# Row factors through memory and residuals without reciprocals in a four-layer graph network

## The chip, the cores and the metric

One core of a Trainium2 chip runs the whole kernel. The metric is device microseconds of one execution, the median over runs; lower is better. TensorE (PE) multiplies into PSUM, VectorE (DVE), ScalarE (ACT) and GpSimd (POOL) work on tiles of 128 partitions, and SyncE (SP) issues most DMAs. Each engine takes its instructions in the order in which they were written; a wait at the head of a queue holds up all that stands behind it.

## What is computed

32 graphs of 256 nodes with 128 features pass four layers. Layers 0 and 1 are graph attention, layer 2 a gated attention by edge type, layer 3 a relational sum. Each layer adds its input to its result and normalizes every node (cut from the reference):

```
def _layernorm(x): return (x - mean(x)) / sqrt(var(x) + 1e-05)
# layers 0 and 1
h = x @ W.T;  s_src = h @ a_src;  s_dst = h @ a_dst
e = leaky_relu(s_src[:, :, None] + s_dst[:, None, :], 0.2)
alpha = softmax(where(adj == 0, -1e9, e), axis=-1)
out = alpha @ h
...
x = _layernorm(x + layer0(x));  x = _layernorm(x + layer1(x))
x = _layernorm(x + layer2(x));  x = _layernorm(x + layer3(x))
```

## The kernel before, in words

The 32 graphs go in 16 pairs (numbered 0 to 15). A pair passes some 40 named steps, and one table, `ORDER`, fixes by hand for each engine in which order it takes the steps of all pairs; `rows0:4` is step "rows" of layer 0 for pair 4. Up to eight pairs are in flight. A second table, `BANKS`, says which of the eight PSUM banks a product of a pair takes; a product waits until the earlier holder of its bank is freed (`freed_by`).

Layers 0 and 1 avoid the softmax over a 256 by 256 matrix of logits. The exponential of a leaky sum is the larger of two products of a row factor and a column factor; what is common to a row or a column is taken out. For a pair the steps are:

- `h` (PE, L1097): the projection, with two more columns that hold the source and destination logits; `logits` (DVE, L811 and L813) copies these two columns to `logit`.
- `gains` (ACT, L609): the exponential of 128x8 logits gives `gain`, a row factor and a column factor for every node.
- `dT` (PE, L1103), `peak` (DVE, L819), `top` (PE, L1107), `dmax` (DVE, L823): the largest destination logit, found by a transposition of 4 columns into a 4x128 row in the bank of `h`.
- `rows` (PE, L1114): four transpositions of a row factor, broadcast along the columns, so that each of the 128 partitions holds the 256 row factors of a graph in PSUM.
- `weight` (DVE, L837): four instructions a pair, each the larger of a row factor from PSUM and a column factor, times the 0/1 mask, into `wgt_all` in SBUF.
- `v`, `vals` (ACT, L615 and L625): the values, with one more column that makes the row sum come out of the same product.
- `out` (PE, L1157): the product of weights and values. Its last column is the row sum.
- `rsum`, `rinv` (DVE, L852, L854, L860): the row sum, held above a tiny number, and its reciprocal; `res` (DVE, L880) adds the product times the reciprocal to the layer's input and frees the bank of `out`.
- `stats` (DVE, L888), `var` (ACT L674, DVE L894 and L898, or POOL L565), `pow` (POOL, L535), `center` (DVE, L902), `norm` (ACT L665 and L668, POOL L549, DVE L793 and L795): the normalization.

Layer 2 has `xTa`, `score`, `sigmoid`, `umax` (L802), `alpha`, `out2` and `res2`; layer 3 has `high`, `low`, `agg`, `out3` and `res3`. POOL adds the biases (`bias`, L530) and forms the low parts (`low`, L541). POOL also issues the mask loads, SP those of `x` and `xT` and the stores of the results. At the end DVE judges flags that would start a general version of the work (`judge`, L910 to L920).

At the start POOL sets a tile of zeros (L515); with it PE runs 5 idle products (L1165, 10 instructions), once the identity matrices are there as well, and then the first projection.

## Time and profile before

| | us |
|---|---|
| median of 3 runs | 253.18 (252.33 to 253.56) |
| profiled execution, its own time | 254.48 |
| its span, first to last instruction | 251.4 |
| busy: PE, DVE, ACT, POOL | 227.2, 229.2, 189.8, 173.4 |
| mean granted clock of PE | 0.982 |
| chain that ended last | PE 55%, DVE 33%, DMA 5%, the rest 7% |

The busy time of a group of instructions is the union of their times, so that where two overlap the time counts once. The mean of a group is that of one instruction, overlap included. Idle time before an instruction is put down to what released it last. The chain that ended last is followed back from the last instruction, at each step to what it waited for.

### The profile page before, as it was taken

How to read it: one execution, taken by the hardware profiler on the slowest of the kernel's cores; microseconds unless marked ns; L12 is line 12 of the kernel's file. 1: busy time of each engine (PE TensorE's matmuls, PEld its weight loads, DVE VectorE, ACT ScalarE, POOL GpSimd, SP SyncE). 2: the span in 40 equal slices, each digit the busy share in tenths (PEclk: the TensorE clock that was granted, in tenths of full speed). 3: DMA queues.
4: the chain of work that ended last, by engine and by line, in shares of the span. 5: the costliest groups of instructions: out<-in, count | busy, mean ns of one | idle time of the engine just before them, and what ended most of it. 6: DMA issues, size and time to landing. Idle time of an engine off the chain costs nothing.

```text
span 251.4 us, 5755 instructions
## 1 busy us (share of the span) xinstructions
PE 227.2 (90%) x1745; PEld 206.6 (82%) x1745; DVE 229.2 (91%) x812; ACT 189.8 (75%) x587; POOL 173.4 (69%) x260
## 2 busy tenths in 40 slices
PE   4998899999999999999999998999999979897850
PEld 4896788987999998988898997989989968776840
DVE  0399989998999999999999999999999888999894
ACT  2497856988968998867998956996891966977752
POOL 6032049878756786789837529984797996699982
PEclk9999999999999999999999999999999979999995
DMA  6999124501452313212230300011000110100106
GB/s 180 252 262 240 52 83 86 126 4 42 83 127 39 88 18 94 104 20 68 54 116 10 117 1 33 14 42 44 1 0 3 42 44 1 43 0 3 42 1 214
DMA packets 12144, 17.56 MB, mean 70 GB/s; under 512 B 1104, under 2 KB 5968, under 8 KB 12112
## 3 DMA queue, kind: packets, MB, share of 16 engines
q1 hardware_dynamic: 9520, 12.85, 16.4%
q0 software_dynamic: 2304, 4.20, 9.9%
q8 instruction: 15, 0.25, 0.4%
q10 hardware_dynamic: 288, 0.14, 0.2%
q14 instruction: 17, 0.14, 0.2%
HBM read 17.17 MB, written 4.19 MB: 85 GB/s over the span
## 4 chain that ended last, share of the span: by engine, by line
PE 55%; DVE 33%; DMA 5%; issue 3%; ACT 2%; POOL 1%; DVEq 0%; SPq 0%; POOLq 0%
PE banks L1157 25%; PE banks L1097 8%; DVE wgt_all L837 7%; PE banks L1124 6%; DVE fstats L888 6%; DMA w<-in_L_gnn_weight 5%; PE banks L1082 4%; DVE fres_all L880 4%; DVE fres_all L868 3%; PE banks L1154 3%; DVE banks L802 3%; PE banks L1114 3%; DVE wgt_all L845 2%; PE banks L1134 2%; PE banks L1107 1%
## 5 line engine op out<-in xcount | busy, mean ns | idle before, releaser
L535 POOL TENSOR_TENSOR frstd<-fvar,minus_half 128x4 f32<-128x4 f32 x64 | 64.8, 1018 | 23.3 <-ACT fvar L674 15.5
L1157 PE MATMUL banks<-vals_all,wgt_all 128*128 128x129 f32 x512 | 63.5, 277 | 3.6 <-ACT vals_all L625 1.9
L1157 PEld LDWEIGHTS banks<-vals_all,wgt_all 128*128 128x128 f32 x512 | 59.6, 191 | 6.6 <-ACT vals_all L625 3.1
L837 DVE SCALAR_TENSOR_TENSOR wgt_all<-banks,gain,mask_all 128x256 f32<-128x256 f32 x128 | 52.6, 471 | 0.3 <-PE banks L1114 0.2
L530 POOL TENSOR_TENSOR xb_all<-xs_all,bias_cen 128x256 f32<-128x256 f32 x62 | 44.5, 737 | 9.5 <-ACT xs_all L668 4.4
L888 DVE BATCH_NORM_STATS2 fstats<-fres_all 128x6 f32<-128x256 f32 x128 | 47.5, 414 | 0.1
L668 ACT ACTIVATE xs_all<-fres_all,frstd 128x128 f32<-128x128 f32 x112 | 35.7, 409 | 0.7 <-POOL frstd L535 0.6
L1157 PE MATMUL banks<-xs_all,wgt_all 128*128 128x128 f32 x256 | 32.7, 283 | 2.6 <-DVE wgt_all L845 2.5
L1157 PEld LDWEIGHTS banks<-xs_all,wgt_all 128*128 128x128 f32 x256 | 30.7, 196 | 3.8 <-DVE wgt_all L845 3.7
L1124 PE MATMUL banks<-fxT,fxTa 128*128 128x256 f32 x128 | 30.3, 381 | 0.0
L605 ACT COPY fxT<-banks 128x256 f32<-128x256 f32 x64 | 20.3, 382 | 12.7 <-PE banks L1082 12.7
L1124 PEld LDWEIGHTS banks<-fxT,fxTa 128*128 128x128 f32 x128 | 23.1, 190 | 2.7
L868 DVE SCALAR_TENSOR_TENSOR fres_all<-banks,xb_all 128x512 f32<-128x512 f32 x32 | 21.5, 679 | 3.5 <-PE banks L1157 2.1
L1114 PE MATMUL banks<-ident,gain 128*128 128x128 f32 x128 | 19.7, 279 | 1.6 <-ACT gain L609 1.2
L802 DVE TENSOR_TENSOR banks<-banks,wgt_all 128x512 f32<-128x512 f32 x32 | 20.9, 687 | 0.3
L641 ACT ACTIVATE wgt_all<-banks 128x512 f32<-128x512 f32 x32 | 19.3, 603 | 2.3 <-PE banks L1124 2.1
L541 POOL TENSOR_TENSOR fxTa<-xs_all,fxTa 128x256 f16<-128x256 f32 x28 | 18.2, 671 | 3.6 <-ACT fxTa L648 3.6
L845 DVE SCALAR_TENSOR_TENSOR wgt_all<-banks,mask_all 128x512 f32<-128x512 f32 x32 | 20.4, 678 | 0.0
L1134 PE MATMUL banks<-mask_all,fxTa 128*128 128x256 bf16 x128 | 16.8, 273 | 3.6 <-POOL fxTa L541 2.1
L1097 PE MATMUL banks<-w_fast,xT_all 128*128 128x130 f32 x128 | 19.4, 299 | 0.5 <-DVE w_fast L740 0.3
L625 ACT ACTIVATE vals_all<-banks,fscale 128x128 f32<-128x128 f32 x64 | 18.1, 377 | 2.0 <-POOL fscale L570 1.1
L642 ACT ACTIVATE banks<-banks 128x512 f32<-128x512 f32 x32 | 19.5, 609 | 0.0
(93 smaller groups left out, 419.2 us busy)
## 6 DMA issues: line engine op xcount, KB each, us to landing
xT_all<-x_turned SPq DMA_DIRECT2D x16, 256.0 KB, 2.9
mask_all<-adj_turned POOLq DMA_DIRECT2D x16, 256.0 KB, 6.0
x_all<-x_laid SPq DMA_DIRECT2D x16, 256.0 KB, 2.8
out<-xs_all SPq DMA_DIRECT2D x16, 256.0 KB, 2.2
bias<-biases_laid SPq DMA_DIRECT2D x1, 128.0 KB, 12.0
w_pack<-W_and_columns ACTq DMA_DIRECT2D x1, 68.0 KB, 3.2
w_fast<-W_turned ACTq DMA_DIRECT2D x1, 64.0 KB, 3.6
w_nat<-in_L_gnn_W SPq DMA_DIRECT2D x1, 64.0 KB, 8.3
```

What stands on the lines that cost most here:

```text
L530: nc.gpsimd.tensor_tensor(xb(u)[:, :, :], xs(u)[:, :, :], bias_cen[:, int(l) - 2, :, :], ALU.add).then_inc(fast_pool[k], 1)
L535: nc.gpsimd.tensor_tensor(frstd[:, int(l), slot(n), :], fvar[:, int(l), slot(n), :], minus_half[:, :, :], ALU.pow).then_inc(fast_pool[k], 1)
L668: last = nc.scalar.activation(xs(u)[:, b, :], fres(u)[:, b, :], ACT.Copy, scale=frstd[:, int(l), u, b:b + 1])
L802: nc.vector.tensor_tensor(scored, scored, wgt(u), ALU.max).then_inc(fast_dve[k], 1)
L837: last = nc.vector.scalar_tensor_tensor(out=wgt(u)[:, c, :], in0=place(f"rows{l}", u), scalar=gain[:, u, c, 1:2], in1=maskT(u)[:, c, :], o ...
L845: nc.vector.scalar_tensor_tensor(out=wgt(u), in0=scored, scalar=1.0, in1=maskT(u), op0=ALU.add, op1=ALU.mult).then_inc(fast_dve[k], 1)
L868: nc.vector.scalar_tensor_tensor(out=fres_all[:, pair(n, FRES), :, :], in0=gathered, scalar={"2": 0.5, "3": 1.0}[l], in1=xb_all[:, pair(n, ...
L888: nc.vector.bn_stats(fstats[:, u, :, :].rearrange("p b k -> p (b k)"), fres(u)[:, :, :].rearrange("p b d -> p d b")).then_inc(fast_dve[k], 1)
L1097: last = nc.tensor.matmul(place(f"h{l}", u)[:, b * HC:(b + 1) * HC], (xT_in if l == "0" else fxT)(u)[:, b * P:(b + 1) * P], w_fast[:, int( ...
L1114: last = nc.tensor.transpose(place(f"rows{l}", u)[:, b * P:(b + 1) * P], gain[:, u, b, 0:1].to_broadcast([P, P]), ident[:, :])
L1124: last = nc.tensor.matmul(place("score", u)[:, c * N:(c + 1) * N], fxTa(u)[:, c * P:(c + 1) * P], fxT(u)[:, :], start=True, stop=True)
L1157: last = nc.tensor.matmul(place(f"out{l}", u)[:, b * width:(b + 1) * width], wgt(u)[:, c, b * P:(b + 1) * P], (vals if l in "01" else xs)( ...
```

## The change

1. **Row factors.** Pairs 3 to 15 no longer use `rows` on PE. `dT` transposes the source logits as well, ACT takes their exponential from PSUM as a 4x128 row (`rowx`), SP writes it to memory (`rowa`, 2 KB) and reads it back for all 128 partitions into `rows_all` in SBUF (`rows` on SP, 256 KB). `weight` reads `rows_all` in the place of a PSUM bank. There are 13 pairs in 2 layers, so 26 such steps, with 52 DMAs on SP.
2. **Residuals.** In layers 0 and 1 the residual is kept times the row sum: input times row sum plus product. `rinv` falls away, and `rsum` in layer 0. The normalization takes the factor out again, if the small constant under its root is multiplied by the squared row sum: ACT forms that square (`sq`, two 128x2 instructions a pair and layer), and `var` on DVE adds it. The bank of `out` is now freed by `sq`.
3. **Start.** DVE sets the zeros, PE waits for them alone and runs 7 idle products. The first four `x` loads wait for `h0`, and the mask loads run 3 pairs ahead, not 6.
4. **New orders** on all engines, new banks, and three places with 5 idle products each on PE (`warm`). Single steps pass to other engines: DVE has `var0` 16 times (before 4), `var2` 5 (1), `var3` 4 (5), `bias3` 3 (1), `norm1` 0 (1), `norm3` 1 (2), `low` 1 (2), `fscale` 4 (5). ACT has `norm1` 6 (8), `norm3` 15 (14), `var3` 9 (2), no `var0` (5). POOL has `norm1` 10 (7), 6 `var` (24), `low` 15 (14), `bias3` 13 (15).

```diff
-AHEAD = 6
+AHEAD = 3
+ROWS, ROW_OUT = 3, 2
...
     "pe": (
-        "h0:0 h0:1 dT0:0 rows0:0 dT0:1 top0:0 top0:1 rows0:1 out0:0 out0:1 turn:0 xT1:0 h0:2 h1:0 xT1:1 dT0:2 dT1:0 "
+        "h0:0 h0:1 dT0:0 rows0:0 turn:0 top0:0 dT0:1 h0:2 rows0:1 dT0:2 top0:1 out0:0 top0:2 h0:4 rows0:2 warm:5 xT1:0 "
...
             def load_x(l, n, k):
                 if n >= X_IN:
                     sp.wait_ge(fast_dve[(n - X_IN) % K], at("dve", "res0", final(n - X_IN)))
+                else:
+                    sp.wait_ge(fast_pe[n], at("pe", "h0", final(n)))
...
+            def send_row(l, n, k):
+                q = SPREAD[l].index(n)
+                sp.wait_ge(fast_act[k], at("act", f"rowx{l}", n * H))
+                sp.dma_start(row_scratch[int(l), n].rearrange("(a d) -> a d", d=P), row_tile(l, n)).then_inc(fast_row_out[int(l)][q % ROW_OUT], 16)
+
+            def spread_rows(l, n, k):
+                q = SPREAD[l].index(n)
+                sp.wait_ge(fast_row_out[int(l)][q % ROW_OUT], 16 * (q // ROW_OUT) + 16)
+                if q >= ROWS:
+                    m = SPREAD[l][q - ROWS]
+                    sp.wait_ge(fast_dve[m % K], at("dve", f"weight{l}", final(m)))
+                sp.dma_start(rows_all[:, int(l), q % ROWS, :], row_scratch[int(l), n].rearrange("(a d) -> a d", a=1).to_broadcast([P, H * N])).then_inc(fast_rows_in[int(l)][q % ROWS], 16)
...
+            def exponential_rows(l, n, k):
+                q = SPREAD[l].index(n)
+                act.wait_ge(fast_pe[k], at("pe", f"dT{l}", n * H))
+                if q >= ROW_OUT:
+                    act.wait_ge(fast_row_out[int(l)][q % ROW_OUT], 16 * (q // ROW_OUT))
+                nc.scalar.activation(row_tile(l, n), place(f"h{l}", final(n))[0:H * NB, 260:260 + P], ACT.Exp, scale=SLOPE - 1).then_inc(fast_act[k], 1)
...
+            def squares(l, n, k):
+                act.wait_ge(fast_dve[k], at("dve", f"res{l}", final(n)))
+                for u in graphs(n):
+                    sums = place(f"out{l}", u)[:, 0:NB * (D + 1)].rearrange("p (b c) -> p b c", b=NB)[:, :, D]
+                    last = nc.scalar.activation(fsq[:, int(l), u, :], sums, ACT.Square, scale=math.sqrt(EPS))
+                last.then_inc(fast_act[k], 1)
...
             def weights(l, n, k):
-                dve.wait_ge(fast_pe[k], at("pe", f"rows{l}", final(n)))
+                spread = n in SPREAD[l]
+                if spread:
+                    q = SPREAD[l].index(n)
+                    dve.wait_ge(fast_act[k], at("act", f"gains{l}", n * H))
+                    dve.wait_ge(fast_rows_in[int(l)][q % ROWS], 16 * (q // ROWS) + 16)
+                else:
+                    dve.wait_ge(fast_pe[k], at("pe", f"rows{l}", final(n)))
...
-                        last = nc.vector.scalar_tensor_tensor(out=wgt(u)[:, c, :], in0=place(f"rows{l}", u), scalar=gain[:, u, c, 1:2],
+                        last = nc.vector.scalar_tensor_tensor(out=wgt(u)[:, c, :], in0=rows_in(l, u) if spread else place(f"rows{l}", u), scalar=gain[:, u, c, 1:2],
                                                               in1=maskT(u)[:, c, :], op0=ALU.max, op1=ALU.mult)
...
-                        last = nc.vector.scalar_tensor_tensor(out=fres(u)[:, b, :], in0=sums[:, b, 0:D], scalar=finv[:, u, b:b + 1],
-                                                              in1=(x_in if l == "0" else fres)(u)[:, b, :], op0=ALU.mult, op1=ALU.add)
+                        last = nc.vector.scalar_tensor_tensor(out=fres(u)[:, b, :], in0=(x_in if l == "0" else fres)(u)[:, b, :],
+                                                              scalar=sums[:, b, D:D + 1] if l == "0" else fsum[:, u, b:b + 1],
+                                                              in1=sums[:, b, 0:D], op0=ALU.mult, op1=ALU.add)
...
-                if l == "1":
-                    nc.vector.scalar_tensor_tensor(out=var, in0=squares, scalar=1 / D, in1=fvar[:, 0, slot(n), :],
+                if l in "01":
+                    dve.wait_ge(fast_act[k], at("act", f"sq{l}", n * H))
+                    nc.vector.scalar_tensor_tensor(out=var, in0=squares, scalar=1 / D, in1=fsq[:, int(l), slot(n), :],
                                                    op0=ALU.mult, op1=ALU.add).then_inc(fast_dve[k], 1)
...
-            pe.wait_ge(ident_set, 2)
-            pe.wait_ge(ident_bf_set, 2)
...
             pe.wait_ge(zero_set, 1)
-            idle_products(5)
+            idle_products(7, 5)
             projection_columns()
+            pe.wait_ge(ident_set, 2)
+            pe.wait_ge(ident_bf_set, 2)
```

**DVE, around the residuals of layer 1 of the first pairs.** `frow`, `fsum` and `finv` are row sums and reciprocals, `fsq` the squares from ACT. Before:

```order
L852 TENSOR_SCALAR frow<-banks 128x2 x2
L819 TENSOR_REDUCE top<-banks 4x1
L860 RECIPROCAL finv<-frow 128x4
L880 SCALAR_TENSOR_TENSOR fres_all<-banks,finv,x_all 128x128 x4
L888 BN_STATS fstats<-fres_all 128x6 x2
L854 SCALAR_TENSOR_TENSOR fsum<-banks,frstd 128x2 x2
L811 COPY logit<-banks 128x4 x2
L860 RECIPROCAL finv<-fsum 128x4
L823 TENSOR_REDUCE minus_dmax<-banks 128x1
L880 SCALAR_TENSOR_TENSOR fres_all<-banks,finv,fres_all 128x128 x4
```

Now:

```order
L890 SCALAR_TENSOR_TENSOR wgt_all<-rows_all,gain,mask_all 128x256 x4
L904 TENSOR_TENSOR fsum<-banks,frstd 128x2 x2
L890 SCALAR_TENSOR_TENSOR wgt_all<-rows_all,gain,mask_all 128x256 x4
L927 SCALAR_TENSOR_TENSOR fres_all<-fres_all,fsum,banks 128x128 x4
L936 BN_STATS fstats<-fres_all 128x6 x2
L904 TENSOR_TENSOR fsum<-banks,frstd 128x2 x2
L943 SCALAR_TENSOR_TENSOR fvar<-fstats,fsq 128x4
L927 SCALAR_TENSOR_TENSOR fres_all<-fres_all,fsum,banks 128x128 x4
L936 BN_STATS fstats<-fres_all 128x6 x2
```

The reciprocals are gone, the weights read `rows_all`, and `var` waits for `fsq` two steps behind its residual.

**SP, from its first DMA to the first rows.** Before:

```order
L468 DMA xT_all<-x_turned 128x512 x2
L463 DMA x_all<-x_laid 128x512 x2
L477 DMA w_nat<-in_L_gnn_W 128x128
L468 DMA xT_all<-x_turned 128x512
L463 DMA x_all<-x_laid 128x512 x2
L468 DMA xT_all<-x_turned 128x512 x2
L477 DMA w<-in_L_gnn_weight 128x128
L477 DMA bias<-biases_laid 128x2x128
```

Now, further on, at the first row factors (pairs 4, 3 and 5 of layer 0):

```order
L483 DMA x_all<-x_laid 128x512 x2
L493 DMA row_scratch<-row_all 4x128
L483 DMA x_all<-x_laid 128x512 x2
L488 DMA xT_all<-x_turned 128x512
L501 DMA rows_all<-row_scratch 128x512
L488 DMA xT_all<-x_turned 128x512
L493 DMA row_scratch<-row_all 4x128
L501 DMA rows_all<-row_scratch 128x512
```

Three loads of 256 KB stand between the first row's way out and its way back.

**PE, from its first instruction.** Before:

```order
L1165 MATMUL banks<-zero 128x128 x5
L1037 MATMUL banks<-w_pack 128x2
L1097 MATMUL banks<-w_fast,xT_all 128x130 x8
L1103 MATMUL banks<-ident,logit 4x128
L1114 MATMUL banks<-ident,gain 128x128 x4
L1103 MATMUL banks<-ident,logit 4x128
```

Now:

```order
L1218 MATMUL banks<-zero 128x128 x7
L1088 MATMUL banks<-w_pack 128x2
L1148 MATMUL banks<-w_fast,xT_all 128x130 x8
L1156 MATMUL banks<-ident,logit 4x128
L1167 MATMUL banks<-ident,gain 128x128 x4
L1094 MATMUL banks<-ident,w_cen 128x128
```

The same work follows two more idle products.

## Rows read from the trace of the kernel before

**Rows 1.** The page's first part: busy us, share of the span, instructions.
```profile
PE 227.2 (90%) x1745; PEld 206.6 (82%) x1745; DVE 229.2 (91%) x812; ACT 189.8 (75%) x587; POOL 173.4 (69%) x260
```
**Rows 2.** Windows: length, then busy PE, PEld, DVE, ACT, POOL, clock, DMA, GB/s.
```profile
125.00:150.00 25.00, 25.00 (x205) 23.51 (x204) 24.82 (x78) 21.59 (x70) 11.73 (x17) 1.00 0.22 64
```
**Rows 3.** Groups by line, DVE: count | busy us, mean ns | idle before, releaser.
```profile
L837 DVE SCALAR_TENSOR_TENSOR wgt_all<-banks,gain,mask_all 128x256 f32<-128x256 f32 x128 | 52.6, 471 | 0.3 <-PE banks L1114 0.2
...
L852 DVE TENSOR_SCALAR frow<-banks 128x2 f32<-128x2 f32 x32 | 3.4, 147 | 0.2 <-PE banks L1157 0.2
...
L860 DVE RECIPROCAL finv<-fsum 128x4 f32<-128x4 f32 x16 | 2.6, 163 | 0.0
L860 DVE RECIPROCAL finv<-frow 128x4 f32<-128x4 f32 x16 | 2.6, 165 | 0.0
```
**Rows 4.** Groups by line, DVE, variances: the same columns.
```profile
L894 DVE SCALAR_TENSOR_TENSOR fvar<-fstats,fvar 128x4 f32<-128x4 f32 x16 | 3.5, 221 | 0.0
...
L898 DVE TENSOR_SCALAR fvar<-fstats 128x4 f32<-128x4 f32 x10 | 2.9, 292 | 0.0
```
**Rows 5.** Groups by line, DVE, steps that pass between engines: the same columns.
```profile
L795 DVE TENSOR_SCALAR xs_all<-fres_all,frstd 128x128 f32<-128x128 f32 x16 | 4.4, 341 | 0.3 <-POOL frstd L535 0.3
...
L775 DVE TENSOR_TENSOR fxTa<-xs_all,fxTa 128x256 f16<-128x256 f32 x4 | 1.8, 476 | 0.0
L793 DVE TENSOR_SCALAR xs_all<-fres_all,frstd,fcenter 128x128 f32<-128x128 f32 x4 | 1.6, 457 | 0.0
```
**Rows 6.** Groups by line, DVE, two inputs from SBUF, and one from PSUM.
```profile
L802 DVE TENSOR_TENSOR banks<-banks,wgt_all 128x512 f32<-128x512 f32 x32 | 20.9, 687 | 0.3
...
L769 DVE TENSOR_TENSOR xb_all<-xs_all,bias_cen 128x256 f32<-128x256 f32 x2 | 0.7, 418 | 0.0
```
**Rows 7.** Timeline at 114 us: start, us, engine, line, operation.
```profile
114.56 1.40 POOL L530 TENSOR_TENSOR xb_all<-xs_all,bias_cen 128x256 f32<-128x256 f32 x2
114.68 0.62 DVE L827 TENSOR_TENSOR fscale<-vals_all,frstd 128x4 f32<-128x4 f32 x1
...
115.36 0.62 DVE L902 SCALAR_TENSOR_TENSOR fcenter<-fstats,frstd 128x4 f32<-128x4 f32 x1
```
**Rows 8.** Instructions of a tile: minimum, median, maximum ns, first and last start.
```profile
L902 DVE SCALAR_TENSOR_TENSOR fcenter<-fstats,frstd x16: 118/154/627, 36.6 to 222.3; 128x4 f32<-128x4 f32 x16
```
**Rows 9.** Windows of line L530 alone, then L541 alone: POOL busy, clock, DMA.
```profile
37.00:241.00 204.00, 44.44 (x62) 0.99 0.18 47
...
37.00:241.00 204.00, 18.20 (x28) 0.99 0.18 47
```
**Rows 10.** Timeline at 113 us: POOL with one tensor input, DVE with two.
```profile
112.64 0.91 POOL L559 TENSOR_SCALAR fxTa<-fxT,w_pack 128x256 f32<-128x256 f32 x1
...
113.03 0.16 DVE L894 SCALAR_TENSOR_TENSOR fvar<-fstats,fvar 128x4 f32<-128x4 f32 x1
```
**Rows 11.** Timeline of the start.
```profile
2.91 2.47 PE L1165 MATMUL banks<-zero 128*128 128x128 f32 x10 [2.91 <-DVE ones_col L723]
...
5.17 0.42 PE L1037 MATMUL banks<-w_pack 128*128 128x2 f32 x2
...
11.06 1.64 DVE L837 SCALAR_TENSOR_TENSOR wgt_all<-banks,gain,mask_all 128x256 f32<-128x256 f32 x4
```
**Rows 12.** Windows, columns as in rows 2.
```profile
205.00:207.00 2.00, 2.00 (x12) 2.00 (x11) 1.30 (x4) 0.00 (x0) 2.00 (x4) 0.50 0.03 8
```
**Rows 13.** Groups by line, PE.
```profile
L1114 PE MATMUL banks<-ident,gain 128*128 128x128 f32 x128 | 19.7, 279 | 1.6 <-ACT gain L609 1.2 <-ACT vals_all L625 0.4
```
**Rows 14.** DMA issues: count, KB each, median us from issue to landing.
```profile
xT_all<-x_turned SPq DMA_DIRECT2D x16, 256.0 KB, 2.9
...
out<-xs_all SPq DMA_DIRECT2D x16, 256.0 KB, 2.2
```
**Rows 15.** Groups by line, ACT.
```profile
L625 ACT ACTIVATE vals_all<-banks,vals_all 128x128 f32<-128x128 f32 x64 | 18.3, 370 | 0.5
...
L674 ACT ACTIVATE fvar<-fstats 128x4 f32<-128x4 f32 x14 | 3.0, 213 | 2.9 <-DVE fstats L888 2.8
```

More of the change, by code:

```diff
@@ L18 @@
 LOGIT_CAP = 24.0
-TINY = 1e-30
+SQUARE_FLOOR = 1e-25
+VARIANCE_CAP = 1e30
 I32 = mybir.dt.int32
@@ L161 @@
 BANKS = {
[13 rows of a table removed]
[13 rows of a table added]
 }
-WHOLE = tuple(n + l for n in ("dT", "top", "gains", "v", "logits", "peak", "dmax", "rsum", "rinv", "var", "center", "pow") for l in "0123") + ("fscale", "seen", "res2", "res3")
+WHOLE = tuple(n + l for n in ("dT", "top", "gains", "rowx", "v", "logits", "peak", "dmax", "rsum", "sq", "var", "center", "pow") for l in "0123") + ("fscale", "seen", "res2", "res3")
 PHASES = {"turn": 1, "h0": H, "rows0": 1, "out0": H, "xT1": 1, "h1": H, "rows1": 1, "out1": H,
@@ L255, with res_gnn_kernel @@
 HELD_BEFORE = holders()
-def res_gnn_kernel(nc, x, adj, W0, a_src0, a_dst0, W1, a1, a2_0, a2_1, a2_2, a2_3, bias2, adj3, W3, bias3, x_laid, x_turned, adj_turned, W0_turned, W0_and_columns, biases_laid, out):
+SPREAD = {l: [n for name, layer, n in order("sp") if name + layer == "rows" + l] for l in "01"}
+def res_gnn_kernel(nc, x, adj, W0, a_src0, a_dst0, W1, a1, a2_0, a2_1, a2_2, a2_3, bias2, adj3, W3, bias3, x_laid, x_turned, adj_turned, W0_turned, W0_and_columns, biases_laid, row_scratch, out):
     B, N, D = x.shape
@@ L477, in load_weights @@
                 sp.dma_start(dst, src).then_inc(signal, 16)
-            steps = {"weights": load_weights, "x": load_x, "xT": load_xT, "store": store}
+            steps = {"weights": load_weights, "x": load_x, "xT": load_xT, "rowa": send_row, "rows": spread_rows, "store": store}
             for step, l, n in order("sp"):
@@ L674, in variances @@
                 nc.scalar.activation(fvar[:, int(l), slot(n), :], fstats[:, slot(n), :, 2], ACT.Copy, bias=floor, scale=factor).then_inc(fast_act[k], 1)
-            steps = {"seen": note_odd, "var": variances, "xT": copy_xT, "gains": gains, "v": exponentials, "vals": values, "xTa": copy_xTa, "sigmoid": sigmoids,
+            def squares(l, n, k):
[4 more added lines that the diff above has]
+                last.then_inc(fast_act[k], 1)
+            steps = {"seen": note_odd, "sq": squares, "var": variances, "xT": copy_xT, "gains": gains, "rowx": exponential_rows, "v": exponentials, "vals": values, "xTa": copy_xTa, "sigmoid": sigmoids,
                      "high": high_part, "agg": copy_gathered, "norm": normalize}
```

89 lines of the change are left out of this document (54 added, 35 removed), and 195 rows, old and new, of tables (BANKS, ORDER).

## The prediction

> **What bounds the kernel now.** I read the page's busy times first, then the windows, then the groups by line. DVE is busy for 229.2 of 251.4 us, PE for 227.2 [rows 1]; in the window from 125 to 150 us both are busy for 24.8 us or more of 25 [rows 2]. The chain that ended last gives most of the span to PE, but with two engines at the limit that says only which of them released the other last. PE's busy time also holds the depth of its pipeline: its transpositions have a mean of 279 ns, and 128 of them fill 19.7 us, 154 ns each [rows 13]. DVE overlaps its neighbours little: 128 weights of 471 ns would be 60.3 us end to end and fill 52.6 [rows 3], 0.06 us of overlap each. So DVE has the least air, and I make the sum on DVE; PE, ACT and POOL are looked at for whether they let DVE run.
>
> The sum is made against the profiled execution: span 251.4 us, its own time 254.48 us, 1.30 us above the median of 253.18. A difference in the span is taken over to the median.
>
> **DVE, removed and added.** Gone are 32 row sums of layer 0 (3.4 us) and 32 reciprocals (2.6 + 2.6) [rows 3]: -8.6 us. The row sums of layer 1 stay. The variances go from 16 + 10 instructions (3.5 + 2.9 us) to 32 of the first kind and 9 of the second, at 0.22 and 0.29 us 7.0 + 2.6: +3.2 [rows 4]. One `norm1` fewer is four instructions (1.6 us), one `norm3` fewer four of 0.275 (1.1 us), one `low` fewer two of 0.45 (0.9 us) [rows 5]; two `bias3` more are four of 0.35: +1.4 [rows 6]. The tile of zeros and two more small instructions in `judge` cost some 0.4 by the short rows. Together -7.2. Short instructions hide up to 0.06 us in their neighbours; 64 go and 15 come, so of 49 times 0.06, 2.9 us, between nothing and all is not really won; I take half, 1.5. **DVE: -5.7 us** (-7.2 to -4.3).
>
> **DVE, the weights from SBUF.** 104 weights (26 steps of 4) now read two tensors in SBUF; before, one came from PSUM. Length by itself: 256 elements with both inputs in SBUF take 418 ns, 512 with one in PSUM 687 [rows 6]. The difference, 269 ns for 256 elements, is 1.05 ns an element; 256 such take 269 ns and leave 149 ns fixed in the one and 150 in the other. I take the weights' own length as unchanged, 0.
>
> The Trainium skill's page "VectorE: DVE Perf Modes", section "The TRN2 errata", has a table that puts the fixed part at 58 cycles from SBUF and 120 from PSUM; by it, as an estimate, the 104 weights would each be 62 cycles shorter, about 65 ns, and the sum 6.7 us lower. The rows above show no such difference, so the trace does not agree with that table.
>
> What the trace does show is a meeting with POOL. While POOL runs its bias additions (two inputs from SBUF), a 128x4 DVE instruction with two inputs from SBUF ends with the first of them, 0.62 us after its start, and the next such one waits out the second, 0.62 us again [rows 7]; the median of that line is 154 ns, its maximum 627 [rows 8]. Beside POOL's one-input L559 a like instruction took 0.16 us [rows 10]. POOL has such two-input work (L530, L541) for 44.4 + 18.2 = 62.6 of the 204 us from 37 to 241: 31% [rows 9], about 0.7 us each. A group of four weights meets one with 31% chance and waits out half of it, 0.35 us: 26 x 0.31 x 0.35 = 2.8 us. Where it was the first of a pair of them (half of the 8 meetings), the second may slip in between two weights: 4 x 0.7 = 2.8, of which I take half. **+4.2 us**, between 0 (no meetings) and 104 x 0.31 x 0.35 = 11.3 (each weight meets POOL for itself). I take the lower part since DVE works through a group without a gap.
>
> **The start.** PE's idle products begin at 2.91 us because PE waits for identity matrices; the projection follows at 5.17, DVE's first weights at 11.06 [rows 11]. With zeros from DVE they can begin up to 1.9 us earlier (1.0 us of 2.91 left for the zeros and their signal, an estimate), and 14 instead of 10 instructions at 0.25 us end at 4.5 instead of 5.4. Against it: on ACT the first `seen`, which waits for a mask, now stands ahead of the first `gains`. Between 0 and -1.9; I take **-1.4 us**, nearer the full distance since PE's work is a chain until the first weights.
>
> **PE's lost clock.** From 205 to 207 us the granted clock is 0.50, the level of 1.2 GHz, 12 products stand in 2 us, and DVE is busy 1.30 of 2.00 [rows 12]; up to 1 us of these 2 is lost. Two of the three `warm` places lie near the end to fill idle time of PE. Between 0 and -1.0; **-0.6 us**, as the stretch may lie elsewhere now.
>
> **PE's relief.** 104 transpositions at 154 ns leave: -16.0 us of busy time [rows 13]. 26 more come back in `dT` (+4.0), and 15 idle products (30 instructions, +4.6), so -7.4. I cost this at nothing: DVE has only 0.18 us of air in 25 [rows 2], so a shorter PE queue has little to give. Its cover is DVE's work; where DVE becomes shorter, PE falls by as much as it.
>
> **ACT.** `rowx` is 26 instructions of 128 elements from PSUM, at 0.29 us 7.4; `sq` is 64 small ones at 0.21, 13.7 [rows 15]. ACT goes from 189.8 to some 210 us, 84% of the span. Beside DVE's work that is hidden; what it costs where it is late stands under the rivals. I take 0.
>
> **The rows' way.** After `dT` a row needs `rowx` (0.29), a way out (nearest row: a store, 2.2) and a way back (nearest: an `xT` load of the same size, 2.9) [rows 14, 15], 5.4 us and two issues on SP. SP stands in line: between them three loads wait for `res0` and `h0` of other pairs. I count on DVE's work between `logits` and `weight` as cover (for pair 4 there stand a weight step, two residual steps and their statistics ahead) and take 0; if that cover fails, each step costs what is missing.
>
> **Sum:** -5.7 + 4.2 - 1.4 - 0.6 = -3.5 us: span 247.9, own time 251.0, median **249.7 us**. A measurement of this kernel can tell about 0.5%, 1.27 us, from no change.
>
> **Rivals.**
> - *The sum without meetings*, 245.5 us: if the weights' groups fall between POOL's additions. For it: the median of rows 8 is untouched. Chance 0.20.
> - *POOL's additions and the weights block each other at every instruction*: +11.3 instead of +4.2, 256.8 us, slower. Place: DVE at L890. From 0.08 us of wait a weight (7.7 / 104) nothing is won. For it: rows 7, where two in a row were held; against it: one of these had another instruction between. Chance 0.15. The Trainium skill's page "SBUF — State Buffer", section "SBUF: two separate sides", states this as an exclusive lock: the Vector instruction with two SBUF inputs or the GpSimd one that starts first holds a shared port pair to its end. Rows 7 agree with it, rows 10 do not, as far as it means every GpSimd instruction.
> - *The rows come late*: if each of the 26 steps lacks 0.2 us, +5.2, 254.9 us; 0.13 a step undoes the win. For it: in-order SP and the crowded DMAs of the first 25 us; against: 16 engines that move little later (share 0.22 in rows 2). Chance 0.13.
> - *ACT is late*: 32 `var` steps on DVE wait for `sq`; at 0.1 us each +3.2, 252.9 us. For it: ACT at 84%; against: most `var` stand one or two steps behind their residual. Chance 0.10.
>
> **How the numbers follow.** The forecast has 0.42, from 247.5 to 251.8. Faster by over 0.5% (below 251.9): the forecast, the sum without meetings, and a part of the late ACT, 0.64. Within 0.5%: most of the late ACT and part of the late rows, 0.16. Slower: the blocking and part of the late rows, 0.20. The range reaches from the sum without meetings, 1 us lower for the start at its best, to just under the blocking: 244.5 to 256.0.
>
> **What would show it.** DVE's busy time near 228 us (229.2 - 5.7 + 4.2); L890 with `rows_all` at a median of 0.47 us and a tenth or so of them near 1 us; L530 with a longer maximum; first weights near 9.7 us; PE near 220, ACT near 210 busy. It is wrong if DVE's idle time before L890 (the rows) or before L943 (the squares) exceeds 2 us in sum, or if the weights' mean moves by over 0.1 us.

## The result, and the profile after

The changed kernel takes **267.62 us** (median of 4 runs, 266.13 to 268.61) against 253.37 for the kernel before on the same chip (4 runs): ratio **1.057**, 95% interval 1.054 to 1.061. That is slower by 5.7%, where 249.7 us (244.5 to 256.0) was forecast. The profiled execution took 266.13 us, with a span of 263.1.

The page of the changed kernel, its busy times, where [rows 1] stand for before:

```profile
PE 224.0 (85%) x1701; PEld 199.0 (76%) x1701; DVE 237.8 (90%) x759; ACT 197.5 (75%) x678; POOL 182.7 (69%) x250
```

DVE was to fall to 228 us and rose to 237.8; POOL rose by 9.3 us, though it has ten instructions fewer. The window from 125 to 150 us of the changed kernel, columns as in [rows 2]:

```profile
125.00:150.00 25.00, 22.39 (x169) 20.06 (x168) 23.87 (x66) 19.74 (x65) 18.16 (x23) 1.00 0.38 96
```

PE had no air there before and now has 2.6 us in 25, and DVE 1.1 instead of 0.2: PE was relieved, and it and DVE now wait. DVE's groups by line in the changed kernel (count | busy us, mean ns of one | idle before and what ended it):

```profile
L890 DVE SCALAR_TENSOR_TENSOR wgt_all<-rows_all,gain,mask_all 128x256 f32<-128x256 f32 x104 | 51.9, 559 | 2.7 <-ACT vals_all L664 1.3 <-issue 0.9 <-DMA rows_all<-row_scratch 0.5
L936 DVE BATCH_NORM_STATS2 fstats<-fres_all 128x6 f32<-128x256 f32 x128 | 47.8, 416 | 0.2
...
L943 DVE SCALAR_TENSOR_TENSOR fvar<-fstats,fsq 128x4 f32<-128x4 f32 x32 | 10.3, 324 | 0.0
L890 DVE SCALAR_TENSOR_TENSOR wgt_all<-banks,gain,mask_all 128x256 f32<-128x256 f32 x24 | 9.8, 477 | 1.4 <-PE banks L1167 1.4
```

The same line 890 has a mean of 559 ns with rows from SBUF and 477 with rows from PSUM (471 before, [rows 3]). The variances, 32 instructions of 4 columns, have 324 ns, and were put at 220 [rows 4]. The views of the tiles that the lines 890, 943 and 562 write, one fence each (minimum/median/maximum ns, first and last start), in the changed kernel:

```profile
L890 DVE SCALAR_TENSOR_TENSOR wgt_all<-rows_all,gain,mask_all x104: 456/477/2280, 28.2 to 223.6; 128x256 f32<-128x256 f32 x104
```

```profile
L943 DVE SCALAR_TENSOR_TENSOR fvar<-fstats,fsq x32: 131/162/1708, 16.9 to 230.5; 128x4 f32<-128x4 f32 x32
```

```profile
L562 POOL TENSOR_TENSOR xb_all<-xs_all,bias_cen x58: 712/723/2213, 48.1 to 252.2; 128x256 f32<-128x256 f32 x58
```

The same views in the kernel before, of the lines 837 and 530:

```profile
L837 DVE SCALAR_TENSOR_TENSOR wgt_all<-banks,gain,mask_all x128: 455/472/486, 11.1 to 205.6; 128x256 f32<-128x256 f32 x128
```

```profile
L530 POOL TENSOR_TENSOR xb_all<-xs_all,bias_cen x62: 713/727/1302, 38.9 to 240.4; 128x256 f32<-128x256 f32 x62
```

The medians of the weights and of the additions are where they were; a few instructions are very long. So nothing became slower as such: some are held up. The timeline of the changed kernel at 171 us (start, us, engine, line, operation) shows one case, POOL's rows first, and at 137 us the worst:

```profile
169.95 1.61 POOL L562 TENSOR_TENSOR xb_all<-xs_all,bias_cen 128x256 f32<-128x256 f32 x2
171.67 1.52 POOL L573 TENSOR_TENSOR fxTa<-xs_all,fxTa 128x256 f16<-128x256 f32 x2
...
171.10 2.77 DVE L890 SCALAR_TENSOR_TENSOR wgt_all<-rows_all,gain,mask_all 128x256 f32<-128x256 f32 x4
...
137.48 3.46 DVE L890 SCALAR_TENSOR_TENSOR wgt_all<-rows_all,gain,mask_all 128x256 f32<-128x256 f32 x4
```

Four weights take 2.77 us where four with rows from PSUM took 1.64 [rows 11]: single ones 0.75, 0.89, 0.89 and 0.47. Here they and POOL's instructions take turns. After each of the first two weights POOL's next instruction goes first, and the next weight waits it out whole. Of the 26 groups of four, 11 hold a weight above 0.56 us (20 weights in all), and these 11 are 8.7 us longer than 1.65 us each. In 7 of them additions and low parts hold the weights: 7.7 us, 1.10 a group. In the other 4 only scalings (line 591) lie beside the long weights: 1.0 us, 0.25 a group.

On POOL's side, two groups of the changed kernel by line:

```profile
L573 POOL TENSOR_TENSOR fxTa<-xs_all,fxTa 128x256 f16<-128x256 f32 x30 | 21.4, 733 | 0.7 <-ACT fxTa L687 0.6
...
L591 POOL TENSOR_SCALAR fxTa<-fxT,w_pack 128x256 f32<-128x256 f32 x18 | 18.7, 1044 | 4.1 <-ACT fxT L637 3.9
```

Low parts had 671 ns and scalings 921 in the kernel before (groups by line, L541 and L559). The chain that ended last went from PE 55% before to this in the changed kernel:

```profile
DVE 39%; PE 16%; POOL 16%; issue 9%; ACT 9%; DMA 8%; SPq 1%; DVEq 0%; POOLq 0%
```

### The profile page after: what moved, and what is told of

Its sections match the earlier page's. It is cut to its first block, busy times and chain, and to the rows that moved or that the text cites. A ratio compares the mean times of both kernels' runs of the same rounds, so it can differ in the third digit from the quotient of the medians.

```text
span 263.1 us, 5826 instructions
## 1 busy us (share of the span) xinstructions
PE 224.0 (85%) x1701; PEld 199.0 (76%) x1701; DVE 237.8 (90%) x759; ACT 197.5 (75%) x678; POOL 182.7 (69%) x250
## 4 chain that ended last, share of the span: by engine, by line
DVE 39%; PE 16%; POOL 16%; issue 9%; ACT 9%; DMA 8%; SPq 1%; DVEq 0%; POOLq 0%
DVE wgt_all L890 12%; PE banks L1210 7%; DVE fres_all L927 7%; POOL frstd L567 7%; DMA rows_all<-row_scratch 6%; DVE fstats L936 5%; POOL xb_all L562 3%; PE banks L1148 3%; DVE wgt_all L898 3%; POOL fxTa L573 3%; DVE fres_all L913 2%; POOL xs_all L581 2%; DMA mask_all<-adj_turned 2%; DVE banks L849 2%; ACT banks L681 2%
## 5 line engine op out<-in xcount | busy, mean ns | idle before, releaser
L567 POOL TENSOR_TENSOR frstd<-fvar,minus_half 128x4 f32<-128x4 f32 x64 | 66.0, 1037 | 23.6 <-DVE fvar L943 18.0
L1210 PE MATMUL banks<-vals_all,wgt_all 128*128 128x129 f32 x512 | 65.3, 279 | 7.2 <-ACT vals_all L664 2.4
L890 DVE SCALAR_TENSOR_TENSOR wgt_all<-rows_all,gain,mask_all 128x256 f32<-128x256 f32 x104 | 51.9, 559 | 2.7 <-ACT vals_all L664 1.3
L936 DVE BATCH_NORM_STATS2 fstats<-fres_all 128x6 f32<-128x256 f32 x128 | 47.8, 416 | 0.2
L1177 PE MATMUL banks<-fxT,fxTa 128*128 128x256 f32 x128 | 31.6, 386 | 1.0 <-DVE fres_all L913 0.9
L546 POOL DMA_DIRECT2D mask_all<-adj_turned x16 | 9.7, 607 | 25.0 <-DVE wgt_all L890 15.2
L573 POOL TENSOR_TENSOR fxTa<-xs_all,fxTa 128x256 f16<-128x256 f32 x30 | 21.4, 733 | 0.7 <-ACT fxTa L687 0.6
L591 POOL TENSOR_SCALAR fxTa<-fxT,w_pack 128x256 f32<-128x256 f32 x18 | 18.7, 1044 | 4.1 <-ACT fxT L637 3.9
L629 ACT ACTIVATE odd_square<-mask_all,minus_half 128x1024 bf16<-128x1024 bf16 x16 | 18.6, 1160 | 3.5 <-DMA mask_all<-adj_turned 3.4
L719 ACT ACTIVATE fsq<-banks 128x2 f32<-128x2 f32 x64 | 7.4, 170 | 17.3 <-DVE fres_all L927 17.2
L581 POOL TENSOR_SCALAR xs_all<-fres_all,frstd,fcenter 128x128 f32<-128x128 f32 x40 | 19.3, 493 | 1.6 <-DVE fcenter L951 1.5
## 6 DMA issues: line engine op xcount, KB each, us to landing
rows_all<-row_scratch SPq DMA_DIRECT2D x26, 256.0 KB, 3.3
xT_all<-x_turned SPq DMA_DIRECT2D x16, 256.0 KB, 3.3
mask_all<-adj_turned POOLq DMA_DIRECT2D x16, 256.0 KB, 3.7
x_all<-x_laid SPq DMA_DIRECT2D x16, 256.0 KB, 2.9
out<-xs_all SPq DMA_DIRECT2D x16, 256.0 KB, 2.1
```

The lines of the kernel that those rows point to most:

```text
L567: nc.gpsimd.tensor_tensor(frstd[:, int(l), slot(n), :], fvar[:, int(l), slot(n), :], minus_half[:, :, :], ALU.pow).then_inc(fast_pool[k], 1)
L573: nc.gpsimd.tensor_tensor(lo(u)[:, :, :], xs(u)[:, :, :], hi(u)[:, :, :], ALU.subtract).then_inc(fast_pool[k], 1)
L581: last = nc.gpsimd.tensor_scalar(xs(u)[:, b, :], fres(u)[:, b, :], frstd[:, 1, u, b:b + 1], fcenter[:, u, b:b + 1], ALU.mult, ALU.add)
L890: last = nc.vector.scalar_tensor_tensor(out=wgt(u)[:, c, :], in0=rows_in(l, u) if spread else place(f"rows{l}", u), scalar=gain[:, u, c, 1:2],
L936: nc.vector.bn_stats(fstats[:, u, :, :].rearrange("p b k -> p (b k)"), fres(u)[:, :, :].rearrange("p b d -> p d b")).then_inc(fast_dve[k], 1)
L1177: last = nc.tensor.matmul(place("score", u)[:, c * N:(c + 1) * N], fxTa(u)[:, c * P:(c + 1) * P], fxT(u)[:, :], start=True, stop=True)
```

## The experiments

Eighteen kernels ran. **Theory A**: DVE's weights, now with all operands in SBUF, and its variances on the one side, POOL's two-tensor instructions on the other hold each other up, and that is the loss. **Rival B**: the rows come late through memory. **Rival C**: the squares on ACT (a variance that waits, a bank that comes free later). **Rival D**: the new order itself. Times beside a ratio are medians; the ratio is to the kernel before, run on the same chip.

### The operand alone: e1, e12, e2

e1, in the kernel before:

```diff
-scalar_tensor_tensor(out=wgt(u)[:, c, :], in0=place(f"rows{l}", u), ...
+scalar_tensor_tensor(out=wgt(u)[:, c, :], in0=sg_all[:, 0, 0, :], ...   # zeros in SBUF
```

> The kernel before, with one operand changed: the weights (line 837) read a fixed SBUF tile of zeros where they read the PSUM bank with the row factors; TensorE still spreads the row factors and the weights still wait for them (so the row factors are left out of the result). Nothing else moves. Theory A (a DVE instruction with two SBUF operands and a POOL instruction with two SBUF operands hold each other up): the weights' mean goes from 0.471 to 0.53 us or more with single ones above 0.9 us, POOL's bias additions from 0.737 to over 0.76 us, and the time from 253.4 to 260 to 270 us. Rival B (the rows' way through memory) and rival C (the squares on ACT) and rival D (the new order): none of them is in this kernel, so the time stays at 252 to 255 us and the weights at 0.46 to 0.48 us.

**269.56 us, 1.067 (1.059 to 1.075).** One operand, moved from PSUM to SBUF in an untouched order, costs 16 us. The page's busy times, the group by line and the view of the line in e1:

```profile
PE 230.1 (86%) x1745; PEld 207.7 (78%) x1745; DVE 243.4 (91%) x813; ACT 190.0 (71%) x587; POOL 181.4 (68%) x260
```

```profile
L840 DVE SCALAR_TENSOR_TENSOR wgt_all<-sg_all,gain,mask_all 128x256 f32<-128x256 f32 x128 | 65.9, 576 | 1.1 <-issue 0.7 <-PE banks L1117 0.3
```

```profile
L840 DVE SCALAR_TENSOR_TENSOR wgt_all<-sg_all,gain,mask_all x128: 461/478/2401, 11.3 to 220.2; 128x256 f32<-128x256 f32 x128
```

DVE's 14.2 us and POOL's 8.0 more are of the size of what the change shows (8.6 and 9.3), with none of B, C and D in it; it has 128 such weights, the change 104. POOL's additions were expected above 0.76 us in the mean; they are at 0.750, so POOL's growth lies elsewhere, in its powers (1.069 us), low parts (0.716) and scalings (0.978).

e12 leaves out TensorE's rows for pairs 3 to 15 as well (no `rows` step in its order; those weights wait for `gains`).

> The run of the kernel before with the weights reading a fixed SBUF tile (269.56 us), and TensorE's spreading of the row factors of pairs 3 to 15 left out as well: 104 products and their weight loads less, some 16 us of TensorE's busy time, and no wait of those weights on them, no way through memory either. If DVE, held up by POOL, sets the end there: 267 to 270 us. If TensorE does: 255 to 262 us.

**267.61 us, 1.057 (1.049 to 1.065)**, with PE at 222.1 us busy and DVE at 242.3. PE's 8 us less buy 2 us, with intervals that overlap: DVE, held up by POOL, sets that time.

e2, in the changed kernel:

```diff
-scalar_tensor_tensor(wgt, in0=rows_in(l, u), scalar=gain, in1=maskT, op0=max, op1=mult)
+tensor_scalar(wgt, rows_in(l, u), gain, 0.5, max, mult)
-scalar_tensor_tensor(var, in0=squares, scalar=1 / D, in1=fsq, op0=mult, op1=add)
+tensor_scalar(var, squares, 1 / D, EPS, mult, add)
```

> The changed kernel; the weights of the pairs whose row factors come through memory are made from the row factors alone, as maximum with the gain times one half (the mask is left out), and the variances of layers 0 and 1 add a constant where they add the squares. Both are then instructions with one SBUF operand; orders, waits and DMAs stay. I expect such a weight to take 0.42 to 0.48 us, as long as the one with two operands. Theory A: no weight over 0.75 us, variances near 0.15 us, DVE busy 222 to 227 us rather than 237.8, POOL's additions back at 0.74 us, and the time 250 to 256 us. Rivals B, C and D: DVE's busy time falls little and the time stays at 262 us or more.

**257.04 us, 1.017 (1.010 to 1.024)**, a little above the 250 to 256 us of theory A, and the reason I gave for it is refuted. The group by line and the view of the line in e2:

```profile
L891 DVE TENSOR_SCALAR wgt_all<-rows_all,gain 128x256 f32<-128x256 f32 x104 | 38.7, 432 | 2.2 <-DMA rows_all<-row_scratch 2.1
```

```profile
L891 DVE TENSOR_SCALAR wgt_all<-rows_all,gain x104: 324/346/936, 30.0 to 214.0; 128x256 f32<-128x256 f32 x104
```

A weight with one tensor operand is held up as much (mean 86 ns above the median, maximum 936). Such a weight is shorter by itself (346 ns), which I had not expected. With that DVE's busy time falls by 11.5 us, to 226.3, and the time by 10.6, while POOL does all of its work. The count of operands is not what decides; that all of them lie in SBUF may be. It can't be that alone: the statistics (L936 above) read and write SBUF too and stayed at 416 ns. The Trainium skill's page "SBUF — State Buffer", section "SBUF: two separate sides", names as VectorE's ways into its lock two SBUF inputs or a performance mode of two ports. The weights of the changed kernel have the first. The 346 ns would fit the second, since they lie 131 ns below the two-input form's 477, half of the 269 ns that 256 elements take by [rows 6]; that the mode was on is not shown here.

### The other suspects in the new order: e3, e6

e3 takes away only the wait of the weights for the rows' DMA (they read a fixed tile):

> The changed kernel; the weights read a fixed SBUF tile of zeros and don't wait for the row factors from memory, while ACT still makes the rows and SP still sends and spreads them (the row factors are left out of the result). Still two SBUF operands. Theory A: the time stays at 263 to 268 us and the weights' mean at 0.54 us or more. Rival B (the rows come late and DVE stands before the weights): the time falls below 259 us.

**264.40 us, 1.044 (1.039 to 1.049)**, weights' mean 555 ns. The rows' lateness is worth 3.2 us of the 267.62: real, and not the cause.

e6 leaves out the squares on ACT; the banks come free with the residual, the variance adds a constant:

```diff
-"out0": (fast_act, "act", "sq0"), ... "out1": (fast_act, "act", "sq1")
+"out0": (fast_dve, "dve", "res0"), ... "out1": (fast_dve, "dve", "res1")
-dve.wait_ge(fast_act[k], at("act", f"sq{l}", n * H))
-scalar_tensor_tensor(var, in0=squares, scalar=1 / D, in1=fsq, op0=mult, op1=add)
+tensor_scalar(var, squares, 1 / D, EPS, mult, add)
```

> The changed kernel, with the squares on ACT left out in the same way: constant in the variance, banks free with the residual. Theory A (operands in SBUF): the variance still meets POOL's additions, so the time stays within 4 us of the changed kernel, 263 to 268 us. Rival C: below 260 us.

**268.41 us, 1.064 (1.058 to 1.070).** Nothing is gained: rival C falls for the new order.

### What the change was to gain: e8, e11, e15, e16, e4, e5

e8 is the kernel before with the change's start (zeros by DVE, seven idle products, identities waited for later):

> The kernel before with the change's start alone: zeros by DVE, seven idle products that wait for the zeros only, the identities waited for after the first projection columns. The x loads are not held back, the masks still run six ahead. My sum gave the start 1.4 us: 251 to 253 us against 253.4. If the masks or x loads set the first weights anyway: 253 to 254 us.

**253.64 us, 1.004 (1.001 to 1.006).** The start gains nothing; if anything it costs 0.9 us.

e11 takes the reciprocals and layer 0's row sums out of DVE's order in the kernel before:

> The kernel before, in which layer 0's row sums and all reciprocals are taken out of DVE's order and the residuals scale the other operand, as in the change; no squares on ACT, variances where and as they were, with a constant (the small term is left out, and layer 1's scale with it). DVE loses 32 x 0.147 + 32 x 0.164 = 10 us of busy time less a little at the residuals and nothing else moves. If DVE sets the end of the kernel before, as my sum took it: 243 to 248 us. If TensorE does, with the rows of all pairs on it: 251 to 254 us.

**252.31 us, 0.996 (0.993 to 0.999).** DVE's busy time fell by 3.9 us (229.2 to 225.3), not by the 8.6 us of the removed groups [rows 3], and the time by 0.4%, about 1 us.

e15 makes one row product per pair in place of four for pairs 4 to 15, and e16 does this and e11 together:

> The kernel before; of the four products that spread a pair's row factors TensorE makes one for pairs 4 to 15, 72 products and weight loads less in all (the rest of those banks holds old numbers, so the weights are wrong), while the weights still read PSUM. It is about what the change takes from TensorE net of its second transposes (104 less 26). If TensorE alone sets the end: 243 to 247 us. If DVE does, or each as soon as the other is relieved: 250 to 253.5 us.

> The same 72 products less, and in addition the reciprocals and layer 0's row sums left out of DVE's order as in the run on the reciprocals alone (252.31 us): both engines relieved at once, in the old order, with the weights reading PSUM; what the change would gain without what it pays. If TensorE and DVE set the end together: 243 to 248 us. If the order's waits do: 250 us or more.

**e15: 252.01 us, 0.995 (0.992 to 0.998). e16: 250.65 us, 0.992 (0.990 to 0.995).** With both engines relieved, the weights still in PSUM, the old order gives 2 us, about the sum of what each relief gives alone (0.4% and 0.5%). The page of e16:

```profile
PE 221.0 (89%) x1673; PEld 198.0 (80%) x1673; DVE 224.1 (91%) x748; ACT 189.6 (77%) x587; POOL 172.9 (70%) x260
```

PE is 6.2 and DVE 5.1 us below [rows 1], and the span of the profiled execution fell by 4.1 (251.4 to 247.3), while the medians differ by 2. Its chain of waits (PE 41%, DVE 40%) crosses from engine to engine; by its mark (250 us or more) the order's waits hold the rest.

e4 and e5 put the change's residuals into the old order, with the rows in PSUM; e4 with the squares on ACT, e5 without:

> The changed kernel's start (zeros on DVE, seven idle products, no wait for the identities; the first x loads are not held back and the masks run six ahead) and its residuals without reciprocals, in the old order and old banks, with the row factors of all pairs spread by TensorE into PSUM as before: from the old tables only the reciprocals, layer 0's row sums and the old variances are taken out, and each square is put on ACT right after its residual, its variance on DVE after it. If the row factors in SBUF are the loss (theory A or B): 246 to 251 us. Rival C (the variance that waits for the square on ACT, and a bank that comes free later, are the loss): 255 us or more, with DVE or PE standing on the squares. Rival D (the new order is the loss): 246 to 251 us as well.

> The run with the old order and the residuals without reciprocals, and in it the squares on ACT left out: the variance adds a constant (the small term times the square of the row sum is left out of the result), and the bank of the sums comes free with the residual again, as in the kernel before. Everything else as in that run (270.97 us). Rival C (the bank that comes free only with ACT's square, and the variance behind it, are what that run lost): 245 to 252 us, and no wait of PE on a square. If C is not the cause, the time stays above 262 us, and the place of the variances on DVE or the start must be it.

**e4: 270.97 us, 1.069 (1.062 to 1.076). e5: 256.94 us, 1.017 (1.013 to 1.020).** In that order the squares cost 14 us without any row in SBUF. The longest waits of PE in e4 (what waits, for what: us in total, times, longest):

```profile
PE banks L1141 <- ACT fsq L712: 5.6, 7, 1.5
PE banks L1203 <- DVE wgt_all L891: 5.2, 4, 3.2
PE banks L1170 <- ACT fsq L712: 2.9, 4, 1.0
PE banks L1126 <- ACT fsq L712: 2.6, 4, 1.0
```

So rival C is a real price that the change's new order avoids: there, PE's waits for the squares are 2.0 and 1.1 us. e5 lies between its two marks, 252 and 262 us, and why it stays 4.6 us above e11 isn't settled; e5 has all variances of layers 0 and 1 on DVE and the new start, and POOL waits 24.5 us for those variances.

### Meetings, POOL's load or the order: e7, e9, e10, e13, e14, e17, e18

e7 and e9 give POOL's additions and low parts the form of its normalizations (one tensor, two scalars, half a tile), with maximum and add in e7, multiply and add in e9:

```diff
-gpsimd.tensor_tensor(xb(u), xs(u), bias_cen[:, l - 2], add)
+for b in range(NB): gpsimd.tensor_scalar(xb(u)[:, b], xs(u)[:, b], bias_cen[..0:1], bias_cen[..1:2], mult, add)
```

> The changed kernel; POOL's bias additions and low parts become instructions with one tensor operand and two scalars on each half of a tile, the form of POOL's normalizations (the bias and the low part are left out of the result). In the trace of the changed kernel no weight that lay beside such a normalization alone took over 0.51 us, while those beside an addition or a low part went to 0.89 to 0.95 us. POOL works longer by it: 58 x (0.89 - 0.79) + 30 x (0.89 - 0.73) = some 11 us. Theory A, in this form (POOL's full-tile instructions with two tensors hold DVE's reading of SBUF up): weights' mean 0.48 us, none over 0.75 us but beside POOL's scaling (L591), variances 0.16 us, DVE busy 223 to 227 us, time 253 to 260 us though POOL does more. If the loss lies elsewhere: 265 us or more.

> The changed kernel with POOL's bias additions and low parts as one-tensor instructions once more, now multiply and add on each half of a tile, which is word for word the operation of POOL's normalizations (0.493 us there), where the last form, maximum and add, took 0.83 us and made POOL the bound (the bias and the low part are left out of the result). Theory A: weights' mean 0.47 to 0.51 us, variances 0.15 to 0.18 us, DVE busy 222 to 228 us, and the time 252 to 260 us, with POOL busy some 12 us longer than in the changed kernel. If the loss isn't in these meetings: 265 us or more with POOL below 200 us busy.

**e7: 324.33 us, 1.281 (1.275 to 1.287)**: the instruction took 0.83 us a half, POOL 260.7 us, and POOL set the time, so e7 says little. **e9: 267.18 us, 1.057 (1.047 to 1.067).** DVE's forecast came true, but for variances of 0.190 us, and the time did not. By its own mark (265 us or more with POOL below 200 us busy) this run speaks against theory A:

```profile
PE 226.0 (86%) x1701; PEld 199.5 (76%) x1701; DVE 226.1 (86%) x759; ACT 198.1 (75%) x678; POOL 198.8 (75%) x338
```

DVE fell by 11.7 us and POOL rose by 16.1. e10 moves the variances of layers 0 and 1 to POOL:

> The changed kernel with the variances of layers 0 and 1 on POOL right ahead of their power (a multiplication and an addition there, 0.2 to 0.25 us each), and none on DVE. POOL can't hold itself up, so the 10.3 us of DVE's variances go and POOL gets 13 to 16 us. Theory A with DVE as the bound: 256 to 262 us. If DVE's time isn't what sets the end of the changed kernel: 266 us or more.

**267.11 us, 1.055 (1.048 to 1.061)**, DVE 229.0 us, POOL 197.0. Again DVE's time went to POOL and the total stayed, at the mark of 266 us for a time that DVE doesn't set. Either POOL's load had become as costly as DVE's, or the order set the time. DVE's waits speak for the first: behind the start DVE stands 9.6 us for POOL's results in e9 and 8.1 in e10, against 2.4 in the changed kernel. The two longest in e9:

```profile
DVE fcenter L955 <- POOL frstd L569: 5.1, 7, 1.2
DVE xs_all L846 <- POOL frstd L569: 3.4, 3, 1.4
```

Two pairs of runs tell more:

```diff
 e13, e14 (changed kernel, kernel before)
-gpsimd.tensor_tensor(xb(u), xs(u), bias_cen, add)
+gpsimd.tensor_tensor(xb(u)[:, :, 0:16], xs(u)[:, :, 0:16], bias_cen[.. 0:16], add)
-gpsimd.tensor_tensor(lo(u), xs(u), hi(u), subtract)
+gpsimd.memset(lo(u), 0.0)
 e17, e18 (changed kernel, kernel before)
-gpsimd.tensor_tensor(frstd, fvar, minus_half, pow)
+gpsimd.tensor_scalar(frstd, fvar, 0.0, 1e-3, mult, add)
```

> The changed kernel; POOL's bias additions cover 16 of the 128 columns of each block and its low parts are zeros written without a read (the rest of the bias sums is zero from the start, so the layers 2 and 3 are not the reference's). Nothing else moves; POOL has some 45 us less to do and hardly anything that meets DVE's weights. Theory A (the meetings set the time in the new order too): weights' mean below 0.49 us, DVE busy 221 to 226 us, time 247 to 256 us. Rival D (the new order, with its waits from engine to engine, sets the time): 261 us or more.

> The same cut of POOL's work in the kernel before, whose weights read PSUM: the control. Theory A: nothing to gain there but POOL's own waits, 249 to 253.5 us. If POOL's load as such sets the time of both kernels: below 248 us.

> The changed kernel; POOL's 64 powers (1.04 us each) become multiply-and-add instructions of about 0.2 us that write a constant (so the normalizations are left out). In the traces a weight beside a power alone took no longer than one beside nothing, so the meetings with additions and low parts stay while POOL gets some 50 us less to do. If the meetings set the changed kernel's time: weights' mean still above 0.54 us, DVE busy above 234 us, time 259 to 266 us. If POOL's load sets it: 248 to 256 us.

> The same in the kernel before, as the control: powers 0.8 us shorter in each chain from a variance to a normalization, POOL 50 us less busy, no meetings to begin with. 247 to 252 us.

**e13: 251.76 us, 0.993 (0.989 to 0.997); e14: 250.45 us, 0.989 (0.984 to 0.994).** Without most of POOL's two-tensor work the changed kernel is 15.9 us faster and its control 2.3; 4 groups of weights are still held beside scalings there, for 1.0 us, as in the changed kernel. **e17: 263.76 us, 1.041 (1.037 to 1.045); e18: 251.23 us, 0.991 (0.988 to 0.994).** With 52 us taken off POOL elsewhere the changed kernel gains 3.9 and its control 2.1. The page's busy times, the view of the weights and the variances' group in e13:

```profile
PE 220.3 (89%) x1701; PEld 198.9 (80%) x1701; DVE 222.1 (89%) x759; ACT 197.3 (79%) x678; POOL 144.5 (58%) x251
```

```profile
L894 DVE SCALAR_TENSOR_TENSOR wgt_all<-rows_all,gain,mask_all x104: 456/476/701, 29.5 to 211.1; 128x256 f32<-128x256 f32 x104
```

```profile
L947 DVE SCALAR_TENSOR_TENSOR fvar<-fstats,fsq 128x4 f32<-128x4 f32 x32 | 5.3, 170 | 0.0
```

The page's busy times and the weights' group in e17:

```profile
PE 225.1 (86%) x1701; PEld 200.9 (77%) x1701; DVE 235.6 (90%) x759; ACT 197.6 (75%) x678; POOL 130.3 (50%) x250
```

```profile
L890 DVE SCALAR_TENSOR_TENSOR wgt_all<-rows_all,gain,mask_all 128x256 f32<-128x256 f32 x104 | 50.2, 540 | 3.2 <-DMA rows_all<-row_scratch 2.5 <-issue 0.7
```

POOL is less busy in e17 than in e13, and DVE is not: its weights are still held. So the meetings are the main part of what the changed kernel loses, and with them in place a smaller load on POOL is worth little. A larger load is not: e9 and e10, with POOL busy for 197 us or more, stay at 267 us though DVE is relieved. How the 15.9 us of e13 divide between the meetings and the 38 us of POOL's work that left with them is not shown; e2, with all of that work in place, is 10.6 us faster. As a cause by itself rival D falls with e13: the same order, the same trip of the rows and the same squares run at 251.8 us. No version here beats the kernel before and computes the reference: e11, e15 and e16, the fastest with POOL's work whole, leave parts of the computation out and gain 0.7 to 2.1 us.

## Why the prediction failed, step by step

**The weights' meetings with POOL (+4.2, 0 to 11.3) is the step that failed most.** The mechanism and its place were right, and [rows 7], which showed it, were read; the size was wrong. The changed kernel is 14.2 us slower (267.62 less 253.37); with POOL's two-tensor work cut in both, they differ by 1.3 (251.76 less 250.45). So the meetings cost some **12.9 us**, as far as the cut of POOL's work is worth the same in both orders. Three parts of the estimate were off:
- "A group of four weights meets one with 31% chance and waits out half of it, 0.35 us": the chance was near, as additions and low parts held 7 of 26 groups, 27%. The price was not: these lost 1.10 us each, where the estimate's 4.2 us over its 8 meetings is 0.53. A group pays for up to three of POOL's instructions. "DVE works through a group without a gap" was the reason for the lower part; in 6 of these 7 groups an instruction of POOL came in between.
- Only line 890 was given meetings. The 32 variances were priced at 0.22 us; they had 0.324, and 0.170 in e13: 5.0 us of busy time from instructions of four columns.
- Only DVE's side was counted. POOL's low parts went from 0.671 to 0.733 us, its additions from 0.737 to 0.786. (Its scalings, 0.921 before and 1.044 now, are at 1.061 in e13 too, so they are no part of the 12.9 us.)

DVE's busy time between e13 and the changed kernel differs by 15.7 us (237.8 less 222.1): 7.7 at the weights (51.9 less 44.2), 5.0 at the variances, 3.0 in the rest. The rival "block each other at every instruction", 256.8 us at 0.15, was nearer, though 15 of the 26 groups were not held: its 11.3 us would have covered the 7.7 at the weights, and its time was too low for the second and third reason and for gains that didn't come.

**DVE, removed and added (-5.7) failed too.** It was said that DVE has the least air, so that what leaves DVE leaves the time. e11 removes 8.6 us of groups, 3.9 of busy time, and 1.0 of time. The allowance for overlap (0.06 us each, half of it taken) was too small: these 64 short instructions filled 0.06 us each, not 0.13. And two engines at 90% of the span are a chain that crosses between them: relieving DVE gave 0.4%, PE 0.5% (e15), both 0.8% (e16). **The start (-1.4)**: the first weights come at 8.41 us in the changed kernel, earlier than the forecast 9.7 and 11.06 before [rows 11]; in e8, with the old x loads, they come at 10.6, and the run gains nothing. Whether the lead of 2.65 us reaches the end of the changed kernel was not tried. Together with the clock's -0.6 the sum held 7.7 us of gains; the control pair shows a loss of 1.3 for all but the meetings. These 9.0 us and the 8.7 of the meetings (12.9 less 4.2) make up the 17.7 by which the result stands above the sum (14.2 less -3.5).

**PE's relief at 0**: 5.9 us less of PE's busy time gave 0.5% (0.2 to 0.8%) in e15, as much as DVE's relief in e11, and e16 about the sum of both. So DVE's lack of air was no reason to cost it at nothing. PE itself is at 224.0 us, not near 220. **ACT at 0**: right in the new order (e6); in the old one 14 us (e4 against e5). That the new order keeps this price away I gave no thought. ACT is at 197.5 us, not 210: a square fills 0.115 us. **The rows' way at 0**: 3.2 us (e3); the mark that I set, over 2 us of idle time before line 890, was passed at 2.7, though only 0.5 of that is put down to the rows' DMA; 6% of the chain lies on it. **The lost clock (-0.6)** wasn't tried by itself.

Of the marks, a tenth or so of the weights near 1 us came true (13 of 104 took 0.84 us or more). Two others read well and misled: line 890's median did stay at 0.477 and its mean moved by less than the 0.1 us that I named as refuting, since 88 ns times 104 is already 9.2 us.

## What to carry to other kernels

Before an operand is moved from PSUM to SBUF on DVE, look at what POOL does meanwhile, and price the meeting at both engines and at every DVE instruction that changes, the short ones too: a four-column instruction can wait as long as a full tile (1.71 us here). A mean that is within 20% of its median hides such a loss; the maximum, and the timeline around it, show it. With two engines at 90%, what leaves one of them is worth a small share of its busy time until a run shows otherwise (3.9 us of DVE gave 1.0 in e11; with DVE held up by POOL, 11.5 gave 10.6 in e2), and short instructions are to be counted by the busy time that they fill.
